# Decoder layer on one core: the experts' down product taken in plain fp32 instead of three rounded passes

## The reference, cut to what matters

```python
logits = einsum('bsd,de->bse', x, router_w) + router_b
top1 = argmax(softmax(logits), axis=-1)
for i in range(8):
    h = einsum('bsd,df->bsf', x, w1[i]) + b1[i]      # 256 -> 2048
    a, g = split(h, 2, axis=-1)
    y = einsum('bsh,hd->bsd', a * sigmoid(g), w2[i]) + b2[i]   # 1024 -> 256
    out = out + where((top1 == i)[..., None], y, 0.0)
```

## Time and profile before

| | |
|---|---|
| median of 3 runs | 1663.69 us (1663.03 to 1664.70) |
| the profiled execution | 1662.15 us, of which the span is 1660.4 us |
| granted TensorE clock, mean over the span | 0.907 |
| trunk, up to about 1160 us | TensorE busy 872 of 1160 us |
| expert tiles, about 1185 to 1595 us | TensorE busy nearly all of it |
| gather and store, to 1660.4 us | no TensorE work |

### The profile page before, as it was taken

One profiled execution on the slowest core, in us unless ns is written; L12 is line 12 of the kernel. 1 busy time (PEld: TensorE's weight loads), 2 busy tenths in 40 slices (PEclk: granted clock), 3 DMA queues, 4 the chain that ended last, 5 costly groups with the idle time before them and its releaser, 6 DMA issues. The chain is left out here.

```text
span 1660.4 us, 24217 instructions
## 1 busy us (share of the span) xinstructions
PE 1280.5 (77%) x8285; PEld 1085.4 (65%) x8285; DVE 957.8 (58%) x1696; ACT 553.9 (33%) x970; POOL 415.5 (25%) x272
## 2 busy tenths in 40 slices
PE   0700579888779888769988799995499999999940
PEld 0400457776657766657766677775499999999940
DVE  0579245667534676634575743332577877878832
ACT  0100212233222332221332233331456666666610
POOL 1356004546202644311635311110000000000034
PEclk9955789999999999989999899998699999999975
DMA  2500000000000000000000000000766676666524
GB/s 59 128 0 0 31 3 15 1 15 15 30 13 12 4 15 15 12 30 1 15 15 15 1 15 15 7 7 7 258 218 209 217 226 207 220 230 199 170 78 138
DMA packets 71010, 118.92 MB, mean 72 GB/s; under 512 B 8992, under 2 KB 61424, under 8 KB 64528
## 3 DMA queue, kind: packets, MB, share of 16 engines
q1 hardware_dynamic: 67776, 109.30, 20.6%
q0 software_dynamic: 3136, 8.39, 1.5%
HBM read 101.09 MB, written 16.58 MB: 71 GB/s over the span
## 5 line engine op out<-in xcount | busy, mean ns | idle before, releaser
L1481 PE MATMUL psH<-xhigh,whigh 128*128 128x256 f32 x736 | 210.9, 287 | 5.7 <-DVE xlow L1331 3.0
L1481 PE MATMUL psH<-xlow,whigh 128*128 128x256 f32 x736 | 208.8, 284 | 0.0
L1481 PE MATMUL psH<-xhigh,wlow 128*128 128x256 f32 x736 | 208.3, 283 | 0.0
L1326 DVE TENSOR_TENSOR wlow<-staged,whigh 128x2048 fp32r<-128x2048 f32 x69 | 157.4, 2282 | 11.5 <-ACT whigh L1400 11.5
L995 PE MATMUL psD<-vo,pT 128*128 128x128 f32 x1024 | 137.7, 283 | 21.1 <-DVE o L747 21.1
L995 PEld LDWEIGHTS psD<-vo,pT 128*128 128x128 f32 x1024 | 128.9, 198 | 32.9 <-issue 25.8
L975 PE MATMUL psA<-qT,kT 128*77 128x256 f32 x512 | 148.6, 389 | 0.0
L1269 POOL DMA_INDIRECT slots<-sorted_y,posi x32 | 31.1, 973 | 456.2 <-DMA sorted_y<-ys 437.4
L1481 PEld LDWEIGHTS psH<-xhigh,whigh 128*128 128x128 f32 x736 | 140.2, 190 | 6.5 <-DVE xlow L1331 3.4
L1400 ACT ACTIVATE whigh<-staged 128x2048 fp32r<-128x2048 f32 x69 | 132.3, 1917 | 32.0 <-DMA staged<-in_L_ffn_w 32.0
L1481 PEld LDWEIGHTS psH<-xlow,whigh 128*128 128x128 f32 x736 | 140.2, 190 | 0.0
(11 more groups left out here) (195 smaller groups left out, 2645.2 us busy)
## 6 DMA issues: line engine op xcount, KB each, us to landing
staged<-in_L_ffn_w SPq DMA_DIRECT2D x69, 1024.0 KB, 5.3
xs<-sorted_x SPq DMA_DIRECT2D x23, 256.0 KB, 2.9
sorted_y<-ys SPq DMA_DIRECT2D x23, 256.0 KB, 2.2
xb<-in_x SPq DMA_DIRECT2D x32, 128.0 KB
out<-slots SPq DMA_DIRECT2D x32, 128.0 KB
xw<-in_x SPq DMA_DIRECT2D x16, 248.0 KB
b2s<-in_L_ffn_b SPq DMA_DIRECT2D x23, 128.0 KB, 3.2
sorted_x<-slots SPq DMA_DIRECT2D x8, 256.0 KB, 2.1
```

The source lines that it names most:

```text
L1326: tt(wlow[par][:, i, :], staged[:, i, :], whigh[par][:, i, :].bitcast(F32), ALU.subtract)\
L1481: ins = mm(psH[:, q % 2 * PAIR + c, part, :], lhs, rhs, start=i == 0, stop=i == len(passes) - 1)
```

## The change

The down product takes the gated values and w2 as they are, in plain fp32, one matmul in place of three. With that go the high and low copies of w2 and of the gated values. w2 is no longer a staged piece: it is loaded by `load_down` into a buffer of its own with two places, `w2s`, with its own semaphores. `gated` now has four places. `down` waits for `gate` itself (`h_done`) instead of the low part. On SP the load of w2 moves from ahead of the wait for `y_done` to behind it, and stands ahead of the output store. The hidden product keeps its three rounded passes.

```diff
-    PIECES = 3
+    PIECES = KC
+        w2s = sb("w2s", [P, 2, HC * C])
-        gated = sb("gated", [P, 2, PAIR, ET])
-        ghigh = sb("ghigh", [P, PAIRS_HID, PAIR, ET], F32R)
-        glow = sb("glow", [P, PAIRS_HID, PAIR, ET], F32R)
+        gated = sb("gated", [P, PAIRS_HID, PAIR, ET])
...
+            def load_down(e, par):
+                src = w2[bass.ds(e, 1)].rearrange("a (k p) n -> p (a k) n", p=P)
+                sp.dma_start(w2s[:, par, :].rearrange("p (k n) -> p k n", k=HC), src).then_inc(w2_in[par], 16)
...
-            load_piece(0, e, KC, wait=False)
+            load_down(e, 0)
...
             for i in range(PIECES):
                 load_piece(1, e, i)
+            load_down(e, 1)
...
+                sp.wait_ge(y_done, t + 2)
                 if exists(t + 2):
-                    load_piece(t + 2, e, KC)
-                sp.wait_ge(y_done, t + 2)
+                    load_down(e, par)
                 sp.dma_start(rows(sorted_y, t), ys[:, par]).then_inc(y_stored[par], 16)
...
             def tile(t, par, turn):            # DVE
-                for q in (2, 3):
-                    gate(t, par, q)
-                    if exists(t + 1):
-                        low_part(t + 1, 1 - par, q - 1)
-                    gate_low(t, q)
+                gate(t, par, 2)
+                if exists(t + 1):
+                    low_part(t + 1, 1 - par, 1)
+                gate(t, par, 3)
                 if exists(t + 1):
                     gate(t + 1, 1 - par, 0)
                     if exists(t + 2):
                         low_tokens(t + 2, par)
-                    gate_low(t + 1, 0)
                     gate(t + 1, 1 - par, 1)
                 finish(t, par, turn)
                 if exists(t + 2):
                     low_part(t + 2, par, 0)
-                if exists(t + 1):
-                    gate_low(t + 1, 1)
...
             gate(0, 0, 0)                      # DVE, before the loop
-            low_part(0, 0, 2)
-            gate_low(0, 0)
             low_tokens(1, 1)
             gate(0, 0, 1)
             low_part(1, 1, 0)
-            gate_low(0, 1)
...
-            high_part(0, 0, KC)                # ACT, before the loop
             act.wait_ge(h_done, 2)
             sigmoids(0, 0, 0, 0)
             high_tokens(1, 1)
-            gate_high(0, 0)
             high_part(1, 1, 0)
             sigmoids(0, 0, 1, 0)
-            gate_high(0, 1)
...
-            def down(t, par, q):
-                pe.wait_ge(g_split, t * PAIRS_HID + q + 1)
+            def down(t, par, q, turn):
+                pe.wait_ge(h_done, t * PAIRS_HID + q + 3)
                 if q == 0:
-                    pe.wait_ge(w_split[KC], t + 1)
+                    pe.wait_ge(w2_in[par], turn * 16 + 16)
                     pe.wait_ge(y_done, t + 1)
                 for c in range(PAIR):
                     k = q * PAIR + c
                     for half in range(2):
-                        for i, (lhs, rhs) in enumerate(((ghigh, whigh), (ghigh, wlow), (glow, whigh))):
-                            ins = mm(psY[:, half, 0:C], lhs[:, q, c, half * P:(half + 1) * P],
-                                     rhs[par][:, KC, k * C:(k + 1) * C],
-                                     start=k == 0 and i == 0, stop=k == HC - 1 and i == 2)
+                        ins = mm(psY[:, half, 0:C], gated[:, q, c, half * P:(half + 1) * P],
+                                 w2s[:, par, k * C:(k + 1) * C], start=k == 0, stop=k == HC - 1)
```

More of the change, by code:

```diff
@@ L1149, in experts @@
         w_split = [sem(f"w_split{i}") for i in range(PIECES)]
+        w2_in = [sem("w2_in0"), sem("w2_in1")]
         bias_in = [sem("bias_in0"), sem("bias_in1")]
@@ L1153, in experts @@
         x_turned, x_high, x_split = sem("x_turned"), sem("x_high"), sem("x_split")
-        h_full, sig_done, h_done, g_high, g_split = (sem(k) for k in ("h_full", "sig_done", "h_done", "g_high", "g_split"))
+        h_full, sig_done, h_done = sem("h_full"), sem("sig_done"), sem("h_done")
         y_full, y_done = sem("y_full"), sem("y_done")
@@ L1179, in load_piece @@
                     sp.wait_ge(w_split[i], t)
[L1180 to L1185, removed]
+                src = w1[bass.ds(e, 1), i * P:(i + 1) * P, :].rearrange("a p n -> p (a n)")
+                sp.dma_start(staged[:, i, :], src).then_inc(w_in[i], 16)
+            def load_down(e, par):
+                src = w2[bass.ds(e, 1)].rearrange("a (k p) n -> p (a k) n", p=P)
+                sp.dma_start(w2s[:, par, :].rearrange("p (k n) -> p k n", k=HC), src).then_inc(w2_in[par], 16)
             def load_bias(e, par):
@@ L1338, in gate @@
                     ins = nc.vector.scalar_tensor_tensor(
-                        gated[:, q % 2, c, :], psH[:, q % 2 * PAIR + c, 0, :], b1s[:, par, q * PAIR + c:q * PAIR + c + 1],
+                        gated[:, q, c, :], psH[:, q % 2 * PAIR + c, 0, :], b1s[:, par, q * PAIR + c:q * PAIR + c + 1],
                         sig[:, q % 2, c, :], ALU.add, ALU.mult)
                 ins.then_inc(h_done, 1)
[L1343 to L1346, removed]
             def finish(t, par, turn):
@@ L1416, in sigmoids @@
                 ins.then_inc(sig_done, 1)
-            def gate_high(t, q):
-                act.wait_ge(h_done, t * PAIRS_HID + q + 3)
-                nc.scalar.activation(ghigh[:, q], gated[:, q % 2], ACT.Copy).then_inc(g_high, 1)
             def tile(t, par, turn):
                 sigmoids(t, par, 2, turn)
-                if exists(t + 1):
-                    high_part(t + 1, 1 - par, 2)
-                gate_high(t, 2)
                 sigmoids(t, par, 3, turn)
-                gate_high(t, 3)
                 if exists(t + 1):
@@ L1433, in tile @@
                         high_part(t + 2, par, 0)
-                    gate_high(t + 1, 0)
                     sigmoids(t + 1, 1 - par, 1, turn + par)
@@ L1437, in tile @@
                         high_part(t + 2, par, 1)
-                    gate_high(t + 1, 1)
             for i in range(KC):
@@ L1500, in tile @@
                 hidden(t, par, 2)
-                down(t, par, 0)
+                down(t, par, 0, turn)
                 hidden(t, par, 3)
-                down(t, par, 1)
+                down(t, par, 1, turn)
                 if exists(t + 2):
@@ L1507, in tile @@
                     hidden(t + 1, 1 - par, 0)
-                down(t, par, 2)
+                down(t, par, 2, turn)
                 if exists(t + 1):
                     hidden(t + 1, 1 - par, 1)
-                down(t, par, 3)
+                down(t, par, 3, turn)
             turn_tokens(0, 0, 0)
```

## The result

The changed kernel takes 1686.15 us in the median (1684.34 to 1687.67), the kernel before 1663.68: 1.0134 times as long, 95% interval 1.0117 to 1.0152. A second measurement gave 1.0136 (1.0121 to 1.0151). The prediction was 1687 us, range 1681 to 1700, slower. The profiled execution is 1685.87 us with a span of 1684.0; forecast were 1685.65 and 1683.9. That the span came within 0.1 us is partly luck, as the end of this text shows.

A forecast was written before the change was run, and what follows sets the result against it. TensorE was taken to bound the tiles. Dearer down quarters 27.4, less 1.8 (start), 1.6 (clock) and 0.5 (end), made +23.5 us: 1685.65 profiled, 1687 as median, range 1681 to 1700.

The forecast's parts named there:

- TensorE alone bounds the tiles: Steady expert tiles: TensorE busy 87.00 of 87.00 us, so DVE and ACT work removed there is worth nothing.
- 0.432 us for a plain matmul: Down product: price taken from the trunk's output projection, 1.728 us a quarter against 1.424, adding 27.4 us in all.
- The count of four passes: Rival, down product: four passes at 0.119 us per plain matmul, 1.90 us a quarter, 1702 us; chance 0.06.
- The start: Before hidden 0 of tile 1: TensorE waits 0.6 us instead of 2.69 and starts 1.8 us sooner.
- clock kept: Behind hidden 0 of tile 1: granted clock stays up after the shorter wait, gaining 1.6 us, held uncertain.
- The end: Last down quarter: TensorE no longer waits for the low part of the gated values, 0.54 us gained.
- SP's queue: Load of w2 moved behind `y_done`: cost zero; rival of a delayed piece 0: 0.8 us a tile, 1704, chance 0.04.
- The margin: SP's queue: piece 0 lands 4.5 us before ACT reads it in the kernel before, enough to cover the moved load.
- A drain at each change: Rival: rounded-plain changes drain TensorE's array, eight a tile at up to 0.16 us, 1716 us; chance 0.06.
- Hidden passes faster for want of traffic: Rival, hidden product: less SBUF traffic lets passes fall to 0.108 us, giving back 23.6 us, 1663.5; chance 0.04.

The follow-up runs named there:

- the splits kept: Changed kernel with high and low parts of w2 and of the gated values computed again but read by nobody; 1687.52 us, 1.0158 of the kernel before.
- The narrow kernels: Kernel before and changed kernel, each with down matmuls of blocks 1 to 6 of 8 cut to 128 output columns; 1654.45 and 1629.40 us.
- narrow rounded kernel: Kernel before with the down matmuls of blocks 1 to 6 of 8 cut from 256 to 128 output columns; 1654.45 us.
- w2 last: Changed kernel with the load of w2 behind the output store, biases and next tile's piece 0 in SP's queue; 1686.55 us, 1.0150 of the kernel before.
- first order: Kernel before, w2 of tile 0 and piece 0 of tile 1 split before the first gate, small operations before the last two tiles; 1662.53 us, 0.9994.
- narrow plain kernel: Changed kernel with the down matmuls of blocks 1 to 6 of 8 cut from 256 to 128 output columns; 1629.40 us.

## Why the prediction was right

**TensorE alone bounds the tiles.** Right: 87.00 busy of 87.00 before, after, and with the splits kept. DVE's fall "to about 43" was worked out with the 4.96 tiles of the old period; the stretch holds 4.63 of the new ones, which makes it 40.5, and 41.26 was measured (42.70 in the second profile, as the stretch cuts the tiles elsewhere).

**0.432 us for a plain matmul.** Right, and it carried the forecast. The trunk's row for another product of the same shape gave 1.728 a quarter, and every down quarter shows 1.73. Over a tile the cost is 1.25 us instead of 1.22: some hidden quarters take 2.87 us in the changed kernel, a few hundredths more than before, which the sum left out. Over the tiles that is about 0.7 us. Why they do isn't shown.

**The count of four passes.** This rival asked for 1.90 a quarter and 1702 us, and 1.73 rules it out. The trace shows two records to a plain matmul, 0.216 us each, and no passes. "FP8 and Floating Point Precision" in the Trainium skill, section "TensorE Precision Notes", gives four passes to true fp32. The trace agrees if a plain pass costs 0.108, where a rounded one costs 0.119. So a count of passes is no price when the two kinds differ. The prediction named that difference without a reason. The narrow kernels give part of it: a rounded pass costs nearly the same at 128 and 256 columns, while a plain matmul halves.

**The start.** Predicted: third gate 1199.95, split of piece 1 at 1200.74, hidden 0 of tile 1 at 1203.26 after 0.6 us, clock kept. Measured: 1199.90, 1200.70, 1203.22, 0.41, clock 1.00. From first hidden to hidden 0 of tile 1 the gain is 20.19 less 18.25, 1.94 instead of 1.8. The matmuls behind it gain 4.47 less 2.97, 1.5 instead of 1.6. Together 3.4; the kernel with the splits kept gives 3.3 once its later rise of the clock is taken off.

That the clock stayed up because the wait was short is not shown. The narrow rounded kernel has the longest wait of all at this place, and no fall behind it:

```profile
1204.97 0.39 PE L1481 MATMUL psH<-xhigh,whigh 128*128 128x256 f32 x1 [2.92 <-DVE wlow L1326]
...
1205.00:1207.00 2.00, 2.00 (x17) 2.00 (x18) 2.00 (x4) 0.63 (x1) 0.00 (x0) 1.00 0.45 94
```

So the length of the wait alone does not decide, and in the prediction these 1.6 us rested on a cause that the traces don't settle. It came true in the three traces with a wait of 0.41 or 0.42 (both of the changed kernel, and w2 last).

**The end.** The last wait is gone. TensorE's last three down quarters in the chain after:

```profile
1614.29 5.19 PE psY L1468 x24
```

5.19 us for three quarters of 1.73 without a gap. The 0.5 us of the sum are the wait that stood there.

**SP's queue.** Zero, as forecast; with the load put last the tiles take the same 434.2 us. The margin did shrink: piece 0 is issued and read here, SP and then ACT:

```profile
1216.96 3.10 SPq L1181 DMA_DIRECT2D staged<-in_L_ffn_w  x2
...
1226.50 1.92 ACT L1389 ACTIVATE whigh<-staged 128x2048 fp32r<-128x2048 f32 x1
```

1216.96 + 6.6 is 1223.6, so 2.9 us are left of 4.5.

**The other rivals.** A drain at each change would have shown as a period of 20; it is 18.78. (The eight changes of this rival count two that the kernel before has too, around the transposes; six are new, a period of 19.7 and about 1709 us in place of 1716.) Hidden passes faster for want of traffic: they are not, neither here nor, in reverse, slower with the splits back.

**How much was luck.** The mechanism held term by term, but the agreement to 0.1 us did not come from it alone. From first hidden to last down the traces differ by 23.9, the main term being 0.7 larger than in the sum and the start and the clock's fall together about what they were. Behind the last down matmul the changed kernel's trace is 0.4 us shorter, and ahead of the first hidden one 0.1 longer, which no term of the sum covers. Between executions of one kernel the time differs by more than that: 3.3 us in the four runs of the changed kernel. The medians differ by 22.5 and 21.8 us in the two measurements; the forecast's 1687 stood 23.3 over the median of before.

## What to carry to other kernels

Before replacing several cheap passes by one exact one, look for the exact form at the same shape elsewhere in the same trace, and take the distance between starts, not the record's duration or a count of passes. Three rounded passes beat plain fp32 at 256 columns (1.43 against 1.73 us a quarter) and lose at 128 (1.29 against 0.89). Removing nearly 40% of the work of two engines that are not the bound gave only what they had held up at the two ends of the pipeline, 3.4 us at the start and 0.5 at the end. Most of that could be had without the change: another order of the start's splits and small operations made the kernel before 0.28% faster.

## What the runs showed of the hardware

A rounded fp32 pass with new 128x128 weights costs 0.119 us at 256 columns and 0.11 at 128. A plain fp32 matmul costs 0.43 and 0.22. Waits of 2.69 and 2.3 us on TensorE at this place (before, splits kept) and one of 2.38 a little earlier (first order) were followed by 3.4 us at the lower level of the granted clock, worth 1.6 us in the kernel before. Waits of 0.28, 0.41, 1.19 and 1.6 us (the last in the narrow plain kernel) were not, and neither was one of 2.92 in the narrow rounded kernel. What decides it stays open.
